# Output norm of the cross-attention branch: two fused VectorE operations in place of four operations on VectorE, ScalarE and GpSimd

## The reference, cut to what matters

```python
def _ln(x, scale, bias):                       # inside the cross-attention
    mu = jnp.mean(x, axis=-1, keepdims=True)
    var = jnp.mean(jnp.square(x - mu), axis=-1, keepdims=True)
    return (x - mu) * jax.lax.rsqrt(var + EPS) * scale + bias
...
    out = out @ Wo
    return _ln(out, lno_s, lno_b)              # the output norm
...
    gate = jax.nn.softmax(xt @ gate_w.T, axis=-1)
    base = xt @ weight.T
    t = jnp.einsum('nh,erh->ner', xt, lora_U)
    lora = jnp.einsum('ne,eor,ner->no', gate, lora_V, t)
    out = base + scaling * lora
...
x = x + _L0_attn_ref(_layernorm(x, axis=-1), ...)
x = x + _L0_xattn_ref(_layernorm(x, axis=-1), ctx_1024, ...)
x = x + _L0_ffn_ref(_layernorm(x, axis=-1), ...)
```

## Time and profile before

| | us |
|---|---|
| median of three runs | 3515.34 |
| profiled execution, span from first to last instruction | 3511.9 |
| TensorE busy in the span | 3335.3 (95%) |
| VectorE busy | 2222.4 (63%) |
| ScalarE busy | 1833.0 (52%) |
| GpSimd busy | 238.9 (7%) |
| first matmul of `feed_forward` to the end of the span | 3314.6 to 3511.9 |

### The profile page before, as it was taken

One profiled execution on the slowest core, in us unless ns is written; L12 is line 12 of the kernel. 1 busy time (PEld: TensorE's weight loads), 2 busy tenths in 40 slices (PEclk: granted clock), 3 DMA queues, 4 the chain that ended last, 5 costly groups with the idle time before them and its releaser, 6 DMA issues. The chain is left out here.

```text
span 3511.9 us, 72470 instructions
## 1 busy us (share of the span) xinstructions
PE 3335.3 (95%) x25084; PEld 2986.2 (85%) x25084; DVE 2222.4 (63%) x4888; ACT 1833.0 (52%) x4388; POOL 238.9 (7%) x324
## 2 busy tenths in 40 slices
PE   6999999998699999999999999999999999999798
PEld 6788888886488989889898898988989889899677
DVE  4666666664565756657575575755757566575487
ACT  4556555654345555555455455545555455454443
POOL 0000000000100000000000000000000000000154
PEclk8999999999799999999999999999999999999899
DMA  5554455445101001010100101101011010100133
GB/s 135 122 126 108 111 131 126 108 106 151 43 27 36 27 26 29 24 36 17 36 29 24 36 17 36 29 24 36 17 36 29 24 36 17 36 12 22 54 120 108
DMA packets 127475, 198.58 MB, mean 57 GB/s; under 512 B 18296, under 2 KB 69240, under 8 KB 126688
## 3 DMA queue, kind: packets, MB, share of 16 engines
q1 hardware_dynamic: 127200, 194.82, 21.1%
HBM read 99.35 MB, written 36.70 MB: 39 GB/s over the span
## 5 line engine op out<-in xcount | busy, mean ns | idle before, releaser
L1279 DVE CUSTOM_DVE_ANT_0 ca_prob<-ca_ps_s,ca_penalty 112x768 f32<-112x768 f32 x512 | 489.9, 957 | 532.8 <-PE ca_ps_s L1110 492.0
L1217 ACT ACTIVATE ca_probT<-ca_ps_t 128x448 f32<-128x448 f32 x512 | 277.7, 542 | 553.9 <-PE ca_ps_t L1121 550.3
L1210 ACT ACTIVATE ca_prob<-ca_prob,ca_low 112x768 f32<-112x768 f32 x512 | 476.6, 932 | 118.7 <-DVE ca_low L1279 114.7
L1095 PE MATMUL ca_ps_f<-ca_wkv_hi,ca_cnT_hi 128*128 128x256 f32 (+1 forms) x1536 | 444.4, 289 | 2.0 <-DVE ca_kstack L1322 2.0
L1095 PE MATMUL ca_ps_f<-ca_wkv_lo,ca_cnT_hi 128*128 128x256 f32 (+1 forms) x1536 | 431.9, 281 | 0.0
L1095 PE MATMUL ca_ps_f<-ca_wkv_hi,ca_cnT_lo 128*128 128x256 f32 (+1 forms) x1536 | 431.2, 281 | 0.0
L1121 PE MATMUL ca_ps_t<-ca_ident,ca_prob 112*128 112x112 f32 x3072 | 407.6, 262 | 1.5 <-ACT ca_prob L1210 0.5
L1121 PEld LDWEIGHTS ca_ps_t<-ca_ident,ca_prob 112*128 112x128 f32 x3072 | 337.4, 140 | 56.6 <-issue 29.9
L1244 ACT ACTIVATE ca_kstack<-ca_ps_f,ca_kbias 64x375 fp32r<-64x375 f32 x512 | 290.2, 567 | 180.0 <-PE ca_ps_f L1095 176.7
L1322 DVE SCALAR_TENSOR_TENSOR ca_kstack<-ca_ps_f,ca_kbias,ca_kstack 64x375 fp32r<-64x375 f32 x512 | 311.3, 608 | 99.2 <-ACT ca_kstack L1244 89.2
L1095 PE MATMUL ca_ps_f<-ca_cnT_lo,ca_wkv_hi 128*128 128x376 f32 x1024 | 342.5, 334 | 27.8 <-issue 27.8
(11 more groups left out here) (218 smaller groups left out, 7061.7 us busy)
## 6 DMA issues: line engine op xcount, KB each, us to landing
ca_q_raw<-q_T SPq DMA_DIRECT2D x128, 224.0 KB, 3.6
ca_cn<-in_ctx_dram SPq DMA_DIRECT2D x16, 1280.0 KB
sa_stack<-sa_qk_hi SPq DMA_DIRECT2D x64, 224.0 KB, 3.1
sa_stack<-sa_qk_lo SPq DMA_DIRECT2D x64, 224.0 KB, 3.5
sa_stack<-sa_qk_lo SPq DMA_DIRECT2D x128, 112.0 KB, 3.2
sa_stack<-sa_qk_hi SPq DMA_DIRECT2D x128, 112.0 KB, 3.0
q_T<-sa_q SPq DMA_DIRECT2D x16, 896.0 KB, 4.5
sa_xn<-in_x_dram SPq DMA_DIRECT2D x16, 448.0 KB, 3.6
```

The lines of the kernel that those rows point to most:

```text
L1095: ins = nc.tensor.matmul(out, lhs[i], rhs[j], start=first_ and n == 0, stop=last_ and n == 2)
L1210: nc.scalar.activation(prob[:, h % 2, q, :], prob[:, h % 2, q, :], ACT.Exp, bias=low[:, h % 2, q:q + 1], scale=-1.0, accum_out=sums[:, h / ...
L1217: nc.scalar.activation(probT[:, h % 2, 2 * u:2 * u + 2, :], src[:, 0:2 * T].rearrange("p (k t) -> p k t", k=2), ACT.Copy).then_inc(TR.done ...
L1279: nc.vector.tensor_tensor_reduce(out=prob[:, h % 2, q, :].rearrange("p (c s) -> p c s", c=2), in0=ps_s[0:QT, :, 0:HALF], in1=penalty[:, :] ...
```

## The change

Two operations of VectorE take the place of `ysh`, `yln`, `ymul` and the plain addition. `ysc` computes ys = (y - mean) * s, and the new `x2` computes x2 = ys * rstd + xb. `ysc` needs no rstd, so it stands ahead of the arrival of that number; `x2` waits for it. The statistics of y and `xb` run one round earlier than before (lead 5 instead of 4). `yst` moves from ahead of `x2` to behind `xst`, and `yeps` moves behind `xeps`. xb gets four buffers, ys two, and the moments of y two. There is one more round before the loop. `load_next` waits for `xb` as well as for ys. VectorE waits for the rows s and b before it starts on the weight parts, because `ysc` reads s. The diff, cut to its core:

```diff
     table = {
         "tensor": [("base", 0), ("gT", 0), ("ug", 1), ("lora", 0), ("xt", 2)],
-        "scalar": [("gexp", 0), ("xt", 1), ("yln", 3), ("xln", 2), ("gT", 0)],
-        "vector": [("xsh", 2), ("xt", 1), ("gt", 0), ("yst", 4), ("x2", 3), ("gT", 0), ("yag", 4), ("xst", 3), ("yeps", 4),
-                   ("xag", 3), ("gmax", 1), ("xeps", 3), ("ysh", 4), ("fin", 0)],
-        "gpsimd": [("ymul", 3), ("xb", 4), ("yinv", 4), ("xinv", 3)],
+        "scalar": [("gexp", 0), ("xt", 1), ("xln", 2), ("gT", 0)],
+        "vector": [("xsh", 2), ("xt", 1), ("gt", 0), ("x2", 3), ("ysc", 4), ("gT", 0), ("xst", 3), ("yst", 5),
+                   ("xag", 3), ("yag", 5), ("gmax", 1), ("xeps", 3), ("yeps", 5), ("fin", 0)],
+        "gpsimd": [("xb", 5), ("yinv", 5), ("xinv", 3)],
     }
...
-        xb = at.sb("xb", [P, 2, D])
-        yn, ys = at.sb("yn", [P, D]), at.sb("ys", [P, D])
+        xb = at.sb("xb", [P, 4, D])
+        ys = at.sb("ys", [P, 2, D])
...
-        stats, moments = at.sb("stats", [P, 2, 6]), at.sb("moments", [P, 2, 2])
-        y_rstd, y_shift = at.sb("y_rstd", [P, 1]), at.sb("y_shift", [P, 1])
+        stats, moments = at.sb("stats", [P, 6]), at.sb("moments", [P, 2])
+        y_stat, y_mom, y_rstd = at.sb("y_stat", [P, 6]), at.sb("y_mom", [P, 2, 2]), at.sb("y_rstd", [P, 4])
...
             LAST = TILES // UNROLL - 1
+            turns(-2, False)
             turns(-1, False)
-            with engine.Fori(0, LAST) as j:
+            with engine.Fori(0, LAST - 1) as j:
                 turns(j, True)
+            turns(LAST - 1, False)
             turns(LAST, False)
...
                     if task == "xb":
                         pool.wait_ge(y_in[p], 2 * DMA * half + 2 * DMA)
-                        nc.gpsimd.tensor_tensor(xb[:, p, :], x1_sb[:, p, :], b_rows[:, :], ALU.add).then_inc(xb_ready, 1)
+                        nc.gpsimd.tensor_tensor(xb[:, v % 4, :], x1_sb[:, p, :], b_rows[:, :], ALU.add).then_inc(xb_ready, 1)
                     elif task == "yinv":
-                        inverse_root(nc, pool, y_rstd[:, :], moments[:, 0, 1:2], minus_half[:, :], y_var, t, y_rstd_ready)
-                    elif task == "ymul":
-                        pool.wait_ge(yn_ready, t + 1)
-                        nc.gpsimd.tensor_tensor(ys[:, :], yn[:, :], s_rows[:, :], ALU.mult).then_inc(ys_ready, 1)
+                        inverse_root(nc, pool, y_rstd[:, v % 4:v % 4 + 1], y_mom[:, p, 1:2], minus_half[:, :], y_var, t, y_rstd_ready)
                     elif task == "xinv":
-                        inverse_root(nc, pool, x_rstd[:, p:p + 1], moments[:, 1, 1:2], minus_half[:, :], x_var, t, x_rstd_ready)
+                        inverse_root(nc, pool, x_rstd[:, p:p + 1], moments[:, 1:2], minus_half[:, :], x_var, t, x_rstd_ready)
...
                 def load_next(t, p):
                     sp.wait_ge(ys_ready, t - 1)
                     sp.sem_inc(sp_passed, 1)
+                    sp.wait_ge(xb_ready, t - 1)
+                    sp.sem_inc(sp_passed, 1)
                     load(t, p)
...
-                    elif task == "yln":
-                        act.wait_ge(y_shift_ready, t + 1)
-                        nc.scalar.activation(yn[:, :], y_sb[:, p, :], ACT.Identity, bias=y_shift[:, :], scale=y_rstd[:, :]).then_inc(yn_ready, 1)
...
             def _(dve):
                 dve.sem_inc(x3_ready, 2)
+                dve.wait_ge(rows_in, 2 * DMA)
                 for s in out_stored:
                     dve.sem_inc(s, DMA)
...
                     if task == "yst":
                         dve.wait_ge(y_in[p], 2 * DMA * half + 2 * DMA)
-                        nc.vector.bn_stats(stats[:, 0, :], y_sb[:, p, :]).then_inc(y_stats, 1)
+                        nc.vector.bn_stats(y_stat[:, :], y_sb[:, p, :]).then_inc(y_stats, 1)
                     elif task == "yag":
                         dve.wait_ge(y_stats, t + 1)
                         dve.sem_inc(dve_passed, 1)
-                        nc.vector.bn_aggr(moments[:, 0, :], stats[:, 0, :]).then_inc(y_moments, 1)
+                        nc.vector.bn_aggr(y_mom[:, p, :], y_stat[:, :]).then_inc(y_moments, 1)
                     elif task == "yeps":
                         dve.wait_ge(y_moments, t + 1)
-                        nc.vector.tensor_scalar(moments[:, 0, 1:2], moments[:, 0, 1:2], XLN_EPS, None, ALU.add).then_inc(y_var, 1)
-                    elif task == "ysh":
-                        dve.wait_ge(y_rstd_ready, t + 1)
-                        nc.vector.tensor_scalar(y_shift[:, :], moments[:, 0, 0:1], y_rstd[:, :], -1.0, ALU.mult, ALU.mult).then_inc(y_shift_ready, 1)
+                        nc.vector.tensor_scalar(y_mom[:, p, 1:2], y_mom[:, p, 1:2], XLN_EPS, None, ALU.add).then_inc(y_var, 1)
+                    elif task == "ysc":
+                        nc.vector.scalar_tensor_tensor(ys[:, p, :], y_sb[:, p, :], y_mom[:, p, 0:1], s_rows[:, :], ALU.subtract,
+                                                       ALU.mult).then_inc(ys_ready, 1)
                     elif task == "x2":
                         dve.wait_ge(ys_ready, t + 1)
                         dve.wait_ge(xb_ready, t + 1)
-                        nc.vector.tensor_tensor(x2[:, v % 4, :], ys[:, :], xb[:, p, :], ALU.add).then_inc(x2_ready, 1)
+                        dve.wait_ge(y_rstd_ready, t + 1)
+                        nc.vector.scalar_tensor_tensor(x2[:, v % 4, :], ys[:, p, :], y_rstd[:, v % 4:v % 4 + 1], xb[:, v % 4, :],
+                                                       ALU.mult, ALU.add).then_inc(x2_ready, 1)
...
```

More of the change, by code:

```diff
@@ L1374, in feed_forward @@
     MIX = ER + NE
-    UNROLL, LEAD = 4, 4
-    assert TILES % UNROLL == 0 and LEAD == UNROLL
+    UNROLL = 4
+    assert TILES % UNROLL == 0
     table = {
         "tensor": [("base", 0), ("gT", 0), ("ug", 1), ("lora", 0), ("xt", 2)],
-        "scalar": [("gexp", 0), ("xt", 1), ("yln", 3), ("xln", 2), ("gT", 0)],
-        "vector": [("xsh", 2), ("xt", 1), ("gt", 0), ("yst", 4), ("x2", 3), ("gT", 0), ("yag", 4), ("xst", 3), ("yeps", 4),
-                   ("xag", 3), ("gmax", 1), ("xeps", 3), ("ysh", 4), ("fin", 0)],
-        "gpsimd": [("ymul", 3), ("xb", 4), ("yinv", 4), ("xinv", 3)],
+        "scalar": [("gexp", 0), ("xt", 1), ("xln", 2), ("gT", 0)],
+        "vector": [("xsh", 2), ("xt", 1), ("gt", 0), ("x2", 3), ("ysc", 4), ("gT", 0), ("xst", 3), ("yst", 5),
+                   ("xag", 3), ("yag", 5), ("gmax", 1), ("xeps", 3), ("yeps", 5), ("fin", 0)],
+        "gpsimd": [("xb", 5), ("yinv", 5), ("xinv", 3)],
     }
@@ L1423, in feed_forward @@
         x_stats, x_moments, x_var = at.sem("x_stats"), at.sem("x_moments"), at.sem("x_var")
-        y_rstd_ready, y_shift_ready, yn_ready, ys_ready = at.sem("y_rstd_ready"), at.sem("y_shift_ready"), at.sem("yn_ready"), at.sem("ys_ready")
+        y_rstd_ready, ys_ready = at.sem("y_rstd_ready"), at.sem("ys_ready")
         x_rstd_ready, x_shift_ready = at.sem("x_rstd_ready"), at.sem("x_shift_ready")
@@ L1501, in _ @@
                 sp.dma_start(b_rows[:, :], lno_b.partition_broadcast(P)).then_inc(rows_in, DMA)
-                AHEAD = LEAD + 2
+                AHEAD = 6
                 for t in range(2, AHEAD):
@@ L1623, in run @@
                         dve.wait_ge(xb_ready, t + 1)
-                        nc.vector.tensor_tensor(x2[:, v % 4, :], ys[:, :], xb[:, p, :], ALU.add).then_inc(x2_ready, 1)
+                        dve.wait_ge(y_rstd_ready, t + 1)
+                        nc.vector.scalar_tensor_tensor(x2[:, v % 4, :], ys[:, p, :], y_rstd[:, v % 4:v % 4 + 1], xb[:, v % 4, :],
+                                                       ALU.mult, ALU.add).then_inc(x2_ready, 1)
                     elif task == "xst":
                         dve.wait_ge(x2_ready, t + 1)
-                        nc.vector.bn_stats(stats[:, 1, :], x2[:, v % 4, :]).then_inc(x_stats, 1)
+                        nc.vector.bn_stats(stats[:, :], x2[:, v % 4, :]).then_inc(x_stats, 1)
                     elif task == "xag":
@@ L1630, in run @@
                         dve.sem_inc(dve_passed, 1)
-                        nc.vector.bn_aggr(moments[:, 1, :], stats[:, 1, :]).then_inc(x_moments, 1)
+                        nc.vector.bn_aggr(moments[:, :], stats[:, :]).then_inc(x_moments, 1)
                     elif task == "xeps":
                         dve.wait_ge(x_moments, t + 1)
-                        nc.vector.tensor_scalar(moments[:, 1, 1:2], moments[:, 1, 1:2], LN_EPS, None, ALU.add).then_inc(x_var, 1)
+                        nc.vector.tensor_scalar(moments[:, 1:2], moments[:, 1:2], LN_EPS, None, ALU.add).then_inc(x_var, 1)
                     elif task == "xsh":
                         dve.wait_ge(x_rstd_ready, t + 1)
-                        nc.vector.tensor_scalar(x_shift[:, p:p + 1], moments[:, 1, 0:1], x_rstd[:, p:p + 1], -1.0,
+                        nc.vector.tensor_scalar(x_shift[:, p:p + 1], moments[:, 0:1], x_rstd[:, p:p + 1], -1.0,
```

## The result

The changed kernel took 3519.43 us (median of 20 runs, 3513.31 to 3525.78), the kernel before 3514.82 (20 runs, 3510.34 to 3519.62). The ratio is 1.0014, with a 95% interval of 1.0008 to 1.0020: 2.8 to 7.0 us slower, 4.9 in the middle, and under the 0.2% that was called no change.

A forecast was written before the change was run, and what follows sets the result against it. No engine is full, so waits set the round, through VectorE's queue. Steady rounds +0.6, start +1.7 and end -0.4 sum to +1.9 us on the median 3515.34: 3517 us, range 3506 to 3526.

The forecast's parts named there:

- The steady round: 22 rounds holding an xb: 6.19 us each against 6.165 before, +0.6 us in all.
- VectorE's own sum: VectorE's queue over one steady round without any block: 5.76 us.
- The block: GpSimd's xb running beside VectorE's x2 lengthens x2 by 0.43 us a round.
- the prediction's algebra: Block B delays ysc, x1's landing and the round alike, so B cancels: x1 lands at 0.41 in the next round.
- the load loop: xb, x2, ysc, load of x1, next xb: x1 lands 3.6 us after ysc ends; round 6.19 us.
- (1) to (4): VectorE's steps from xsh to the next xsh: 1.17 + 1.32 + 0.21 + 0.60 + 2.46 = 5.76 us.
- The price of the fused form: x2 and ysc on VectorE: 0.69 + 0.05 = 0.74 us each when unblocked.
- rival B: x1's load lands later with store issued behind fin; from 0.23 us a round, +7 us, counted slower; chance 0.13.
- rival C: yinv held up on GpSimd by fin, lengthening the wait for xinv; at 0.4 us a round, 3526; chance 0.06.
- The start: Up to gT_lo of tile 0: +1.7 us; +3.0 if xb 3 gets between x2 1 and ysc 2.
- The total: Whole run: +1.9 us, 3517 us on the median.
- the end: The last xb is in round 22, so round 23 is 0.43 shorter: -0.4 us.

The follow-up runs named there:

- experiment 4: Changed kernel with xb computed on 32 of 512 columns, the other 480 left as zeros; ratio 0.9981 to the kernel before.
- 5: Changed kernel with four buffers for y and x1 instead of two; ratio 0.9987 to the kernel before.
- experiment 2: Changed kernel with VectorE's wait for the rows s and b put behind the nine weight parts; ratio 1.0003 to the kernel before.
- experiment 3: Changed kernel with xinv ahead of yinv in GpSimd's list; ratio 0.9999 to the kernel before.
- 6: Kernel before the change with xb ahead of ymul in GpSimd's list; ratio 1.0004 to the unedited kernel before.
- 8: Kernel before the change with xb ahead of ymul and four buffers for y and x1; ratio 0.9943 to the unedited kernel before.
- 1: Changed kernel with ysc ahead of x2 in VectorE's list; ratio 0.9986 to the kernel before.

## Why the prediction was right

**The steady round** was forecast at 6.19 us and measured at 6.191. Two of its parts were off and cancelled. VectorE's own sum is 5.69 us (experiments 4 and 5), not 5.76: `yeps` stands 1.04 behind `yst`, where I had 1.15, since behind `yag`, `gmax` and `xeps` take steps of 0.05 to 0.09 and not 0.1 each. The block is 6.191 - 5.69 = 0.50, not 0.43. That they cancel is no luck: the prediction's algebra said that the block makes up the difference to the load loop, whatever VectorE's sum is. Had I written the loop down by itself (`xb` 1.29, `x2` to 0.55 behind it, `ysc` 0.66, 3.6 for the load: 6.1), the sum of (1) to (4) wouldn't have been needed.

**The price of the fused form** was right: 0.74 us in the trace against 0.74, from one row with a scalar per row at twice the length.

**The load and the store** (rival B): x1 landed 2.9 us after its issue as before, so the later store did no harm. Single loads that landed later are told of in the last section. **yinv held up by `fin`** (rival C) did not happen: 0.55 in the steady rounds.

**The start** was the term that was mis-sized: +3.0 us in place of +1.7. The prediction had both ends and chose the wrong one: `xb` 3 did get in between `x2` 1 and `ysc` 2, for 1.0 us of block. Another 0.5 stands ahead of the first `yst`: the first weight part begins 7.33 us into the stage, not 3320.98 - 3313.89 = 7.09, and the parts take 3333.25 - 3328.90 = 4.35 us, not 4.1, with 0.43 of waiting for ScalarE in them. The remaining steps came out 0.2 shorter than walked. That the block is part of the start is borne out by experiment 4, where with `xb` cut short the start is 1.7 us less.

**The total**: +3.4 us in the stage by the traces, +4.9 (2.8 to 7.0) by the runs, +1.9 forecast. Of the 3.0 between the forecast and the runs' middle, 1.3 are the start and 0.2 the end, forecast at -0.4 and measured at -0.2. The last 1.5 lie outside the stage. Whether the new code does that was not tested by itself: if I take the stage from the median of each experiment's kernel, what is left differs from that of the kernel before by -2.2 to +2.9 us, so 1.5 can't be told from nothing.

**The block.** A fused operation beside `xb` is lengthened, and not when `xb` is cut short (experiment 4). It goes in the other direction too: beside `ysc`, `yinv` takes 0.99 us instead of 0.55 in the start of experiment 2,

```profile
3326.81 0.74 DVE L1618 SCALAR_TENSOR_TENSOR ff_ys<-ff_y,ff_y_mom,ff_s_rows 128x512 f32<-128x512 f32 x1
```

```profile
3326.97 0.99 POOL L166 TENSOR_TENSOR ff_y_rstd<-ff_y_mom,ff_minus_half 128x1 f32<-128x1 f32 x1 [1.76 <-DVE ff_y_mom L1616]
```

and ends at 3327.96, 0.41 behind `ysc`. A blocked fused operation ends 0.55 us behind GpSimd's, though alone it takes 0.74, so 0.19 us of it lie under the block. The Trainium skill, page "SBUF — State Buffer", section "Who interferes with whom", has a VectorE instruction with two SBUF inputs and a GpSimd one that reads SBUF contend, and has the loser wait for the whole of the other instruction. The traces agree on the first, for the fused form too, and not fully on the second: by it the fused operation would end 0.74 behind `xb`.

## What to carry to other kernels

Look for loops that run through a transfer: who issues the load, what must have been read first, and who waits for what lands. In such a loop a wait that is taken away can come back as a longer block (experiment 3), or a block as a wait (6), and two edits that are worth nothing alone can be worth 20 us together (8). Ask of a more compact form of the arithmetic whether the arithmetic is on that loop; here the buffers and the order of the lists decided, and the old and the fused form came out level.

## What the runs showed that I had not expected

Some loads land late, and what that costs depends on where `xb` then falls. In the 21st of the 22 rounds of the changed kernel, x1 landed 3.7 us after its issue instead of 2.9, while the queue that fetches instructions moved one packet of 0.02 MB. The transfers in that stretch:

```profile
q8 instruction: 1, 0.02, 0.9%
...
ff_x<-x SPq DMA_DIRECT2D x1, 256.0 KB, 3.7
```

`xb` then met `x2` half way and held up `ysc` instead:

```profile
3483.31 0.74 DVE L1624 SCALAR_TENSOR_TENSOR ff_x<-ff_ys,ff_y_rstd,ff_xb 128x512 f32<-128x512 f32 x1
3483.55 1.64 POOL L1473 TENSOR_TENSOR ff_xb<-ff_x,ff_b_rows 128x512 f32<-128x512 f32 x1 [1.46 <-DMA ff_x<-x]
3483.97 1.77 DVE L1618 SCALAR_TENSOR_TENSOR ff_ys<-ff_y,ff_y_mom,ff_s_rows 128x512 f32<-128x512 f32 x1
```

`xb` itself waits for `x2` (1.64 us), then `ysc` for `xb` (1.77): a chain of two blocks, and a round of 6.70 us. In experiments 1 and 2 there is one such round too (6.71 and 6.70), at the same place, with a load that took 4.6 and 3.7 us and the same packet beside it.

But a late load need not cost anything. In the first of the 22 rounds of the changed kernel x1 took 4.8 us. `xb` came behind both fused operations:

```profile
3360.07 0.74 DVE L1624 SCALAR_TENSOR_TENSOR ff_x<-ff_ys,ff_y_rstd,ff_xb 128x512 f32<-128x512 f32 x1
3360.73 0.75 DVE L1618 SCALAR_TENSOR_TENSOR ff_ys<-ff_y,ff_y_mom,ff_s_rows 128x512 f32<-128x512 f32 x1
3361.44 1.29 POOL L1473 TENSOR_TENSOR ff_xb<-ff_x,ff_b_rows 128x512 f32<-128x512 f32 x1 [2.59 <-DMA ff_x<-x]
```

Neither was blocked, and the round took 5.67 us, half a microsecond less than the others. In experiment 3 x1 took 3.8 us at the place of the long round, and the round took 5.15. In experiment 4, with `xb` cut short, x1 took 3.7 us there and the round 5.69, as all the others; with four buffers none of the 22 is over 5.69. So, as far as these traces show, what costs time is the block, and the load sets what is blocked. In the changed kernel the short round and the long one cancel in the mean: the other twenty average 6.19. That the fetch of instructions is what makes a load late was read from the timing alone; no run took the fetch away.
